# Pairs of weighed scan states added by accumulating DMAs, and half a B product moved between two engines, in a Mamba plus mixture-of-experts kernel

## The reference, cut to what matters

```python
def _selective_scan(u, delta, A, B, C, D):
    deltaA = jnp.exp(jnp.einsum('bld,dn->bldn', delta, A))
    deltaBu = jnp.einsum('bld,bln,bld->bldn', delta, B, u)
    ...
    def step(h, inputs):
        dA_t, dBu_t, C_t = inputs
        h = h * dA_t + dBu_t
        y = jnp.einsum('bdn,bn->bd', h, C_t)
        return (h, y)
    ...
    return y + u * D
...
y = _selective_scan(xs, delta, A, B, C, D)
y = y * jax.nn.silu(res)
out = y @ W_out + x
```

## Time and profile before

| | us |
|---|---|
| median of 3 runs | 1617.81 (1616.9 to 1623.03) |
| the profiled execution | 1620.9 |
| its span from first to last instruction | 1618.9 |
| busy in it: PE, DVE, POOL, ACT | 1449.8, 1308.3, 1077.6, 741.5 |

### The profile page before, as it was taken

How to read it: one execution, slowest core, us unless ns; L and a number is a source line. 1 busy time by engine, 2 the same in 40 slices (tenths; PEclk the granted TensorE clock), 3 DMA queues, 4 the chain that set the end, 5 groups by cost and what they waited for, 6 DMA issues and landing times. The chain is left out here.

```text
span 1618.9 us, 14732 instructions
## 1 busy us (share of the span) xinstructions
PE 1449.8 (90%) x4412; PEld 725.0 (45%) x4413; DVE 1308.3 (81%) x1931; ACT 741.5 (46%) x1160; POOL 1077.6 (67%) x545
## 2 busy tenths in 40 slices
PE   6578998889998889998798878899998999999996
PEld 3233443334443334443343323444445766667774
DVE  4599999999999999999999997355636777777772
ACT  4566665776656776657566664421000111111111
POOL 0199898999887999989999997230011455555453
PEclk9889999899999999999899999999999999999998
DMA  4540112410113411103310004021412888888895
GB/s 131 221 174 9 42 48 101 179 40 30 35 47 108 171 41 36 35 15 126 129 36 21 28 1 156 20 104 33 182 54 64 225 237 225 218 239 223 259 260 68
DMA packets 63823, 176.86 MB, mean 109 GB/s; under 512 B 10304, under 2 KB 15168, under 8 KB 55040
## 3 DMA queue, kind: packets, MB, share of 16 engines
q1 hardware_dynamic: 48128, 138.59, 24.8%
q0 software_dynamic: 15616, 37.32, 11.1%
HBM read 142.98 MB, written 32.85 MB: 109 GB/s over the span
## 5 line engine op out<-in xcount | busy, mean ns | idle before, releaser
L1342 POOL TENSOR_TENSOR h<-h,c_rep 128x2048 f32<-128x2048 f32 x128 | 579.3, 4530 | 31.2 <-DVE h L945 26.1
L1542 PE MATMUL bank<-h,ident 128*128 128x512 f32 x916 | 449.3, 634 | 93.0 <-POOL h L1342 74.2
L717 ACT ACTIVATE bank<-delta,a_neg 128x512 f32<-128x512 f32 x512 | 335.8, 682 | 178.9 <-DVE h L945 178.1
L1542 PEld LDWEIGHTS bank<-h,ident 128*128 128x128 f32 x916 | 180.6, 202 | 335.9 <-issue 210.9
L945 DVE TENSOR_TENSOR_SCAN h<-bank,state,h 128x512 f32<-128x512 f32 x256 | 306.0, 1260 | 0.5 <-ACT bank L717 0.5
L945 DVE TENSOR_TENSOR_SCAN h<-bank,h 128x512 f32<-128x512 f32 x256 | 290.7, 1199 | 2.8 <-ACT bank L717 2.6
L171 DVE STREAM_TRANSPOSE xT<-xg 32x256 f32<-32x256 f32 (+1 forms) x592 | 247.3, 418 | 56.0 <-DMA xg<-flat,slot_token 48.3
L935 DVE TENSOR_TENSOR h<-bank,b_rep 128x2048 f32<-128x2048 f32 (+1 forms) x105 | 227.5, 2184 | 35.7 <-ACT bank L708 24.2
L1703 POOL DMA_INDIRECT out<-y,slot_token x64 | 101.8, 1590 | 110.1 <-DMA out<-y,slot_token 65.2
L1329 POOL TENSOR_TENSOR h<-du,b_rep 128x2048 f32<-128x2048 f32 (+1 forms) x32 | 125.4, 3920 | 11.5 <-PE bank L1542 11.5
L1787 ACT ACTIVATE y<-y_ps,share 128x512 f32<-128x512 f32 x69 | 47.4, 687 | 185.3 <-PE y_ps L1935 152.3
(11 more groups left out here) (238 smaller groups left out, 1530.0 us busy)
## 6 DMA issues: line engine op xcount, KB each, us to landing
w_ring<-in_w SPq DMA_DIRECT2D x32, 1024.0 KB, 5.3
b_rep<-bcd SPq DMA_DIRECT2D x16, 1024.0 KB, 6.9
c_rep<-bcd SPq DMA_DIRECT2D x16, 1024.0 KB, 5.0
w_ring<-in_w SPq DMA_DIRECT2D x32, 512.0 KB, 7.4
w_in<-in_w_in_x SPq DMA_DIRECT2D x32, 256.0 KB, 2.6
w_res<-in_w_in_res SPq DMA_DIRECT2D x32, 256.0 KB, 2.6
xa<-in_x SPq DMA_DIRECT2D x20, 256.0 KB, 3.0
xb<-in_x SPq DMA_DIRECT2D x16, 256.0 KB, 3.0
```

The lines of the kernel that those rows point to most:

```text
L717: eng.activation(da[j][:], delta[:, g % 2], ACT.Exp, scale=a_neg[:, col:col + 1])\
L1342: ins = eng.tensor_tensor(h[:, q], h[:, q], c_rep[:, Q * q:Q * q + Q, :], ALU.mult)
L1542: ins = eng.matmul(y_ps[:], c.ident[:], h[:, q, j, :], start=False, stop=(q == NQ - 1 and j == Q - 1))
```

## The change

Three things change.

- The pairwise add of a folded quarter is no longer a POOL instruction. POOL issues a DMA from SBUF to SBUF that adds `h[q, 2:4]` onto `h[q, 0:2]` (128 partitions by 1024 float32, 512 KB). Ahead of it POOL waits for its own weighing, and for the landing of the DMA before the last one (two semaphores in turn). PE waits for the landing where it waited for POOL.
- Quarters 0 and 1 of dense slots are now folded too, in this way. Leaving slots keep their three. That makes 27 DMAs in place of 27 POOL adds, and 18 new ones.
- In leaving slots POOL makes half of the B product of quarter 3, which DVE made in whole. In the slots that follow a leaving one (9, 10, 11, 17, 18, 19, 25, 26, 27) DVE makes the B product of quarter 2 behind the scans of quarter 1, no longer ahead of them.

```diff
         def by_pool(g, q):
 
+            if q == NQ - 1:
+                return (Q // 2, Q) if leaving(g) else (0, Q)
             if leaving(g):
                 return (0, 0)
-            if q == NQ - 1:
-                return (0, Q)
             return (Q // 2, Q) if q == NQ - 2 and dense(g) else (0, 0)
...
-            return leaving(g) and q < NQ - 1
+            return leaving(g) and q < NQ - 1 or dense(g) and q < NQ // 2
+
+        folds = [(g, q) for g in range(LAST + 1) for q in range(NQ) if folded(g, q)]
+
+        def fold_of(g, q):
+
+            n = folds.index((g, q))
+            return fold_landed[n % 2], 16 * (n // 2 + 1)
...
                     scans(g, 0)
                     if d == 6:
                         statistics(s + 2, (0, 1))
-                    spread(g, 2)
+                    late = g > 0 and leaving(g - 1)
+                    if not late:
+                        spread(g, 2)
                     scans(g, 1)
+                    if late:
+                        spread(g, 2)
...
-                    ins = eng.tensor_tensor(h[:, q], h[:, q], c_rep[:, Q * q:Q * q + Q, :], ALU.mult)
+                    eng.tensor_tensor(h[:, q], h[:, q], c_rep[:, Q * q:Q * q + Q, :], ALU.mult).then_inc(S["cmul_done"], 1)
                     if folded(g, q):
-                        ins.then_inc(S["weighed"], 1)
-                        weighed[0] += 1
-                        eng.wait_ge(S["weighed"], weighed[0])
-                        ins = eng.tensor_tensor(h[:, q, 0:Q // 2], h[:, q, 0:Q // 2], h[:, q, Q // 2:], ALU.add)
-                    ins.then_inc(S["cmul_done"], 1)
+                        landed, count = fold_of(g, q)
+                        after(eng, landed, count - 16)
+                        eng.wait_ge(S["cmul_done"], g * NQ + q + 1)
+                        eng.dma_start(h[:, q, 0:Q // 2, :], h[:, q, Q // 2:, :], accum_op=ALU.add).then_inc(landed, 16)
...
-                    eng.wait_ge(S["cmul_done"], g * NQ + q + 1)
+                    if folded(g, q):
+                        eng.wait_ge(*fold_of(g, q))
+                    else:
+                        eng.wait_ge(S["cmul_done"], g * NQ + q + 1)
```

More of the change, by code:

```diff
@@ L233, in front @@
                  "conv_chain xs_ready bcd_written sp_chain sp_ready delta_ready "
-                 "du_made du_ready bq_made b3_made da_ready scan_done state_saved weighed cmul_done y_summed gate_done "
+                 "du_made du_ready bq_made b3_made da_ready scan_done state_saved cmul_done y_summed gate_done "
                  "xr_ready").split()
         S = {n: sem("m_" + n) for n in names}
+        fold_landed = [sem(f"m_fold_landed{u}") for u in range(2)]
         b_loaded = [sem(f"m_b_loaded{q}") for q in range(NQ)]
@@ L1341, in weigh @@
                         eng.wait_ge(S["state_saved"], (s // 2 * DC + d) * NQ + q + 1)
-                    ins = eng.tensor_tensor(h[:, q], h[:, q], c_rep[:, Q * q:Q * q + Q, :], ALU.mult)
+                    eng.tensor_tensor(h[:, q], h[:, q], c_rep[:, Q * q:Q * q + Q, :], ALU.mult).then_inc(S["cmul_done"], 1)
                     if folded(g, q):
-                        ins.then_inc(S["weighed"], 1)
-                        weighed[0] += 1
-                        eng.wait_ge(S["weighed"], weighed[0])
-                        ins = eng.tensor_tensor(h[:, q, 0:Q // 2], h[:, q, 0:Q // 2], h[:, q, Q // 2:], ALU.add)
-                    ins.then_inc(S["cmul_done"], 1)
-                weighed = [0]
+                        landed, count = fold_of(g, q)
+                        after(eng, landed, count - 16)
+                        eng.wait_ge(S["cmul_done"], g * NQ + q + 1)
+                        eng.dma_start(h[:, q, 0:Q // 2, :], h[:, q, Q // 2:, :], accum_op=ALU.add).then_inc(landed, 16)
                 for s in (0, 1):
```

## The result

| | before | after |
|---|---|---|
| median us (lowest to highest), 4 runs each, same chip | 1619.96 (1616.9 to 1623.03) | 1693.83 (1685.37 to 1697.54) |
| profiled execution: time / span us | 1620.9 / 1618.9 | 1693.75 / 1691.7 |
| mean granted clock of TensorE | 0.963 | 0.943 |

The changed kernel is slower: 1.0449 times the time before, 95% interval 1.0403 to 1.0494. Forecast was 1642, so +24 us; it became +74. The time lies above the range.

A forecast was written before the change was run, and what follows sets the result against it. Touched slots were taken as bound by DVE or POOL work, dense slot 20 also by a four-engine loop. Losses of 23.2, 1, 7 and 3 us less 10 gained gave +24: 1642 us, range 1610 to 1676.

The forecast's parts named there:

- the loop through four engines: Dense slot 20: DVE scans, POOL weighings, PE sum and projection, ACT tap, back to DVE; 31.64 us becoming 36.7.
- last rival: Dense-slot chain isn't the bound, so PE's relief would gain 10 us and more; held within quick issue's 12%.
- c: POOL's time for one DMA issue, wait included: taken as 1.3 us, ends 0.1 to 1.9.
- L: Time from the end of a POOL weighing to the DMA's landing: taken as 5.5 us, ends 3.4 to 8.0.
- The clock: Half clock on PE after waits: four dense-slot cases, 7 us, plus 3 us for the leaving slots' sums.
- leaving slots' own loop: Leaving slots: scans 0 through POOL's half product, landing and sum 1 to B product 1; 27.2 us (27.7 even), tying DVE.
- quarter 2 lands before the late B product 2: After leaving slots: 17.9 us of DVE work behind scans 2 hides fold 2's landing, so no wait.
- Slots 3, 11, 19: Dense slots where POOL comes in late: landing delays sum 1, projection and tap by 3.3 us each, 9.9 lost.
- Slots d = 5: Dense slots 5, 13, 21, no "in" item behind quarter 1: loop 29.7 against 29.2 us; 1 us lost.
- Quick landing: Rival: L = 3.4 and c = 1.3, net +3 us, 1621, no change; 13%.
- quick issue: Rival: issue costs POOL 0.1 us and landing takes 3.4; leaving slots gain 16 us, 1606; 12%.
- slow landing: Rival: L = 8.0 and c = 1.9, +82 us, 1700; 17% for all from 1662 up.

The follow-up runs named there:

- e6: e1 with four zero matmuls on PE ahead of each landing wait in dense slots: 1662.14 us (1660.71 without one run of 3095.24).
- e1: Changed kernel with leaving slots put back as before, so only the 18 dense DMA folds remain: 1674.14 us, ratio 1.0341.
- e12: Changed kernel with zero matmuls on PE ahead of landing waits, four in dense slots, two ahead of fold 2 in leaving slots: 1671.86 us.
- e3: e2 with all of quarter 3's B product in leaving slots back on DVE: 1630.25 us, ratio 1.008.
- e10: Kernel before, with only quarters 0 and 1 of leaving slots folded by DMA and quarter 2 summed whole by PE: 1615.28 us.
- e2: Changed kernel without the dense folds, so only the leaving slots' part of the change remains: 1643.91 us, ratio 1.0173.
- e4: Changed kernel with PE running the "in" projection ahead of a folded quarter's sum in dense slots: 1654.5 us, ratio 1.0233.

## Why the prediction was off

**What was right.** *The bound of the dense slots* was read rightly from the earlier trace rows: the loop through four engines, closed before, longer after. Slots 3 and 11 had another bound, though: PE was busy there for all of the 34.7 and 33.4 us before, which the prediction named only in its last rival. *c* was taken at 1.3 and is about 1.5: 0.55 of wait for POOL's own weighing, 0.61 from the issue to the next instruction, and some 0.3 by which that next one is longer (4.82 in place of 4.53, 1.57 in place of 1.27). *L* was taken at 5.5: from 741.08 to 746.78 is 5.7, with the 0.55 of wait in it, and the line of the 45 issues gives from issue to landing

```profile
DMA to landing us min/median/max: 4.5/4.6/7.1
```

The Trainium skill (DMA: Bandwidth & Descriptors, "Anatomy of one DMA") would give an estimated 3.2 us for these 512 KB; the quickest of 45 took 4.5, so the trace does not agree, and the rows of scatters and gathers were the better guide. The term for slots 4, 12 and 20 (+13.3) is what e6 shows: 110.0 against 96.4, +13.6.

**The clock was mis-sized: 10 us forecast.** The earlier trace rows show a wait of 2 us and half clock behind it, and I counted four such places at 1.7 us. In the changed kernel 36 waits for a landing end on PE, and time at half clock grew by 82 us. Kept busy by matmuls of zero, the whole kernel is 22 us faster, e1 13. Two things were missed. It is not only the wait ahead of sum 1 of six slots that counts: all nine dense slots have a granted clock of 0.84 to 0.92, where seven of them had 1.00 before. And the slots behind them lose as well. 72 us at half clock remain in e12, about the 68 of before, so little of what the change added is left in it; whether the fillers cost time themselves no run tells.

**The leaving slots had the wrong sign: -10 forecast, +13.7 measured**, and more behind them. The prediction had named longer leaving slots as a sign of being wrong, and they are longer. The step that failed is the leaving slots' own loop. I followed B product 3 on POOL only forward, to weighing 1 and landing, and did not ask what it waits for itself: sum 3 of the slot before. The earlier trace rows had this in view, in the same tile and line: the halves of POOL's B product waited for PE's sum already. The second error is "quarter 2 lands before the late B product 2". The landing was compared with DVE's use alone; PE's queue in between, where sum 2 holds the gate projection and sum 3 behind it, was left out. e3 less e10 puts 15 us on this one, e2 less e3 13.7 on the first.

**Slots 3, 11, 19: +9.9 forecast, +22.1 measured.** Slot 3, which has no leaving slot ahead, is +3.9 with the clock held (e6), near the 3.3. In the changed kernel it is +6.6. Slots 11 and 19 were to gain up to 3 us from a POOL that had caught up; it had not, as the rows of slots 9 to 10 show. For them e6, where the leaving slots are as before, still has +7.7 and +5.8. In slot 11 of e6 fold 1 landed 5.9 us after its issue (5.0 in slot 4), and the sum behind it ran at half clock (3.64 us for 1.98): some 2.6 of the 4.4 us above the forecast. I have no row that divides the rest.

**Slots d = 5: +1 forecast, +7.6 measured.** With PE filled, 13 and 21 are at +0.1 and +0.4, as the loop gave (0 and 0.5). Slot 5 is at +4.4 there. POOL's issue of its fold 1, sum 1 on PE and the next B product on DVE, in e6:

```profile
249.47 0.88 POOL L1367 DMA_DIRECT2D h<-h  x1 [0.56 <-POOL h L1356]
256.31 3.78 PE L1567 MATMUL bank<-h,ident 128*128 128x512 f32 x4 [3.61 <-DMA h<-h]
260.13 2.29 DVE L944 TENSOR_TENSOR h<-bank,b_rep 128x2048 f32<-128x2048 f32 x1 [4.08 <-PE bank L1567]
```

The landing took 6.8 us from the issue, 1.8 more than in slot 4, while the other queues moved 786 KB; beside none of the other 17 was it over 270. The fillers were too short for it, and the sum took 3.78 us for 1.98. With the forecast 0.5 that is 4.1 of the 4.4. The slowest landing of the changed kernel (7.1 us, slot 13) had 786 KB beside it too. One L for all landings hid this; that the traffic is the cause was not tested.

**The other slots: nothing forecast, +15.6 measured.** They are those behind the changed ones. e2 has +4.7 of it, e1 +12.1, e6 +6.0: so about half of the dense folds' share goes with the clock. That the rest is an engine that comes late out of a longer slot is my reading, which no run singles out.

**The rivals.** Quick landing, quick issue and slow landing were all about c and L, and these came out at the middle. "Slow landing" gave 1700, near the truth for a reason that is not there. That folded sums could hold PE's queue in leaving slots was among no rival, and the range was built of c, L and a small clock term alone. That is why it was too narrow.

**What stays open.** The time outside the scan stage is 1 to 12 us shorter in the traces of the other thirteen kernels than in that of before, though they are the same there; and part of slots 11 and 19 of e6.

## What to carry to other kernels

A transfer put in place of an add is not free because the queue that issues it has room: its landing falls to whoever waits, and to all that stands behind that wait in order. Put what doesn't need the landing ahead of the wait (e4: 39 us with one reordering). And before an operation is moved to another engine, list what it waits for there as carefully as what waits for it.

## What the runs showed of the hardware

- An accumulating DMA within SBUF, 128 partitions by 4 KB, lands 4.5 to 7.1 us after its issue, median 4.6, at 45 issues. In the 19 of them beside which other queues moved under 10 KB it was 4.5 to 4.8; the slowest, 7.1, had 786 KB beside it. It costs GpSimd about 1.5 us of its time when it must wait for its own last instruction, of which 0.3 appears as a longer next instruction.
- Waits of 3 to 4 us on PE, twice in a slot, took the granted clock of slot 4 from 1.00 to 0.91 and of slot 20 from 1.00 to 0.87 in the changed kernel; sum 1 behind such a wait took 3.6 and 3.8 us in place of 1.9. Matmuls by zero ahead of the wait, with 1.76 us of it left, kept the clock of slot 4 at 1.00; they made e1 13 and the whole changed kernel 22 us faster.
